# Four attention layers in a row: layers of different batches mixed on every engine, and the full layers' values in fp32

## The reference

```python
def L0(x):   # 32-wide queries and keys, full attention
    Q, K, V = Wq x + bq, Wk x + bk, Wv x + bv
    return gamma * (V @ softmax(Q K^T)^T) + x
def L1(x):   # and L3: 32 groups, 256-wide queries and keys
    h = group_norm(x) * g + b
    q, k, v = wq h + bq, wk h + bk, wv h + bv
    return x + wo (v @ softmax(q^T k / 16)^T) + bo
def L2(x):   # tokens: xs = x as (1024, 256)
    x_ln = ln(xs); q = 8 heads of 32, * 32 ** -0.5; k, v = 32 wide, shared by the heads
    sim = where(causal, -max, q k^T)
    av = ln(softmax(sim) v @ wo + xs)
    ff = gelu(ln(ln(av) @ w1 + b1)) @ w2 + b2
    return ff + av
x = L3(L2(L1(L0(x))))
```

## Time and profile before

| | |
|---|---|
| runs | 1568.68, 1571.64, 1576.68 us |
| the profiled execution | 1572.43 us, its span 1570.7 us |
| TensorE busy | 1326.2 us (84%) |
| VectorE busy | 1008.6 us (64%) |
| ScalarE busy | 567.8 us (36%) |
| GpSimd busy | 122.8 us (8%) |
| DMA | 27.20 MB, 17 GB/s on average |

### The profile page before, as it was taken

The page is one execution under the profiler, slowest core; times in us unless marked ns, Lnnn a source line. Parts: engine busy times, 40 slices in busy tenths (PEclk is TensorE's granted clock), DMA queues, the critical chain, the costliest instruction groups (busy, mean ns, idle before and its releaser), DMA issues.

```text
span 1570.7 us, 21594 instructions
## 1 busy us (share of the span) xinstructions
PE 1326.2 (84%) x7440; PEld 999.4 (64%) x7440; DVE 1008.6 (64%) x1913; ACT 567.8 (36%) x777; POOL 122.8 (8%) x314
## 2 busy tenths in 40 slices
PE   5789888958978988984998898896798898889688
PEld 4568664547866865444876776544686687645577
DVE  2647568666565756866656565877575565696665
ACT  2324224514342423452434331452343242245143
POOL 0000011210000001121000000212000000112100
PEclk9789979989979987997998997998798899799699
DMA  4000110000000011000000003000000001100000
GB/s 140 1 27 1 41 42 2 2 1 1 29 1 27 1 44 39 2 1 1 1 29 1 27 0 82 2 1 1 1 1 29 1 1 38 45 1 2 1 1 27
DMA packets 16393, 27.20 MB, mean 17 GB/s; under 512 B 2576, under 2 KB 6800, under 8 KB 16272
## 3 DMA queue, kind: packets, MB, share of 16 engines
q1 hardware_dynamic: 16272, 25.66, 5.9%
HBM read 8.61 MB, written 4.19 MB: 8 GB/s over the span
## 4 chain that ended last, share of the span: by engine, by line
issue 88%; POOL 7%; PE 4%; POOLq 0%; DVE 0%; ACT 0%
PE ring L589 3%; POOL cprobs L560 3%; POOL rstd L544 2%; POOL idle_pool L559 2%; PE ring L670 0%; POOLq L426 0%; PE ring L738 0%; POOLq L543 0%; PE ring L743 0%; ACT h_hi L974 0%; DVE x L1174 0%; POOLq L547 0%; DVE gn_nb L1250 0%; DVE gn_msc L1249 0%; DVE gn_sc L1248 0%
## 5 line engine op out<-in xcount | busy, mean ns | idle before, releaser
L1030 ACT ACTIVATE cprobs<-ring 128x1024 f32<-128x1024 f32 (+1 forms) x192 | 152.1, 812 | 206.3 <-PE ring L855 205.8
L589 PE MATMUL ring<-probsT_hi,vt_hi 128*128 128x512 f32 x384 | 158.2, 412 | 11.9 <-DVE probsT_lo L1120 11.6
L918 ACT ACTIVATE probsT_hi<-ring 128x1024 fp32r<-128x1024 f32 x96 | 98.1, 1026 | 188.4 <-PE ring L670 188.0
L1120 DVE TENSOR_TENSOR probsT_lo<-ring,probsT_hi 128x1024 fp32r<-128x1024 f32 x96 | 116.5, 1221 | 67.0 <-ACT probsT_hi L918 67.0
L831 PE MATMUL ring<-ks,qs 96*128 96x512 f32 (+3 forms) x384 | 144.0, 452 | 17.9 <-DVE part_max L1375 6.1
L589 PE MATMUL ring<-probsT_hi,vt_lo 128*128 128x512 f32 x384 | 153.9, 401 | 0.0
L589 PE MATMUL ring<-probsT_lo,vt_hi 128*128 128x512 f32 x384 | 153.6, 400 | 0.0
L1375 DVE TENSOR_REDUCE part_max<-ring 128x2 f32<-128x1024 f32 (+3 forms) x128 | 127.3, 1017 | 35.1 <-PE ring L835 17.2
L855 PE MATMUL ring<-qs,ks 98*128 98x512 f32 (+3 forms) x384 | 115.6, 396 | 13.6 <-DVE part_max L1375 12.1
L544 POOL TENSOR_TENSOR rstd<-var_eps,half_neg 128x2 f32<-128x2 f32 (+1 forms) x52 | 46.2, 889 | 997.8 <-DVE var_eps L1245 548.1
L926 ACT ACTIVATE probs<-ring,neg_max 128x1024 f32<-128x1024 f32 x96 | 106.8, 1113 | 42.0 <-DVE neg_max L1154 38.8
(11 more groups left out here) (218 smaller groups left out, 2592.3 us busy)
## 6 DMA issues: line engine op xcount, KB each, us to landing
qs<-q_hi SPq DMA_DIRECT2D x64, 128.0 KB, 2.3
xin<-x_dram SPq DMA_DIRECT2D x4, 1024.0 KB, 5.1
qs<-q_lo SPq DMA_DIRECT2D x32, 128.0 KB, 2.3
out_dram<-x SPq DMA_DIRECT2D x8, 512.0 KB, 2.9
qs<-max_rows SPq DMA_DIRECT2D x64, 4.0 KB
raw_L_wv<-L_wv_dram SPq DMA_DIRECT2D x2, 256.0 KB, 6.2
raw_L_woT<-L_woT_dram SPq DMA_DIRECT2D x2, 256.0 KB, 6.3
raw_L_wq<-L_wq_dram SPq DMA_DIRECT2D x2, 256.0 KB, 6.6
```

Of the source, the lines that this page charges most:

```text
L589: ins = mm(out, w, m, start=first and n == 0, stop=last and n == len(every) - 1)
L918: A(dst, flat(name) if src is None else src, ACT.Identity, bias=bias, scale=scale).then_inc(hi_ready, 1)
L1030: A(causal_probs(step, two, n), slot(event_name(e))[:, :, 0:n], ACT.Exp).then_inc(act_read, 1)
L1120: ins = v.tensor_tensor(dst, src, f32(hi), ALU.subtract)
```

## The change

- **Two chains.** The loop over batches is gone; all work is written out. The *full chain* is the preparation of L0's weights and 12 full layers, in the order of `FULL`, so that full layers of one batch stand beside the causal layer of another. The *causal chain* is the rest of the preparation and the 4 causal layers. On each engine both chains are generators, and a string of `ORDER` says which goes on next (`F` or a digit for a step of the full chain, `C` or a letter for one of the causal; on TensorE digit and letter also give the PSUM bank).
- **PSUM** is 7 single banks that both chains take by these letters, and one bank of sums for the causal values.
- **Values of full layers in fp32.** `vt` and `probsT` are no longer split. `full_values` works in quarters of 256 queries: 2 channel tiles by 8 key tiles, one fp32 product of 256 columns each, 64 for each layer. VectorE's low halves of both are gone; ScalarE copies the transposed tile once.
- **Scaling** of the tiles is done by ScalarE in 9 of the 12 full layers (`SCALED_BY`, `scaled`), by VectorE in 3.
- **Causal layer** in 8 blocks of 256 queries by 4 heads, all 4 heads in one exponent. The feed-forward part is in 4 token parts of 256 (3 before). Each block has its own stack of 12 transfers of 32 partitions by 256 queries; there are 4 places for stacks.
- **Start.** The input is loaded behind L0's weights; the other weights are loaded and prepared in the causal chain, beside the first full layers.

On SP, before, the first transfers of a causal layer are those of the first half of the queries, both groups of heads at once: 12 transfers; 12 more follow for the second half (the last row is their first), and then the first maxima.

The diff, cut to its core (the kernel's other helpers are rewritten as generators around the same instructions):

```diff
+FULL = [("L0", 0), ("L1", 0), ("L0", 1), ("L1", 1), ("L0", 2), ("L3", 0), ("L1", 2), ("L0", 3), ("L3", 1), ("L1", 3),
+        ("L3", 2), ("L3", 3)]
...
+SCALED_BY = ["dve" if n in (0, 1, 11) else "act" for n in range(len(FULL))]
...
+ORDER = {
+    "PE": (
+        "0F2eF02F4Fg02F40Fg24F02FFF3F50F24FFF5F02e6FFF0c3FFF64F024F0F2404F20F42F06FFF4F20F46FFF2F04c6FFF06FFFec0F4F0c"
...
+    events = [("xt", 0), ("xt", 1), ("xn", 0), ("q2", 0), ("kv", 0), ("vt", 0)]
+    events += max_events(0) + max_events(1) + [("shift", 0), ("shift", 1)]
...
+def weave(order, full, causal):
+
+    for ch in order:
+        next(full if ch in "F0123456" else causal)
...
-                    wait_read(sp, b, event_name(("q2", ib)))
...
-                        for g, src in enumerate((q2[0], q2[0], q2[1])):
-                            sp.dma_start(qs[DH * g:DH * (g + 1), ib, a::4, :].bitcast(F32),
-                                         src[DH * a:DH * (a + 1), :, sl].bitcast(F32)).then_inc(stack_in[ib][a // 2], 16)
...
+            def stacks(b, k):
+                hg, qi = BLOCKS[k]
+                wait_read(sp, f"C{b}.q2{qi // 2}")
+                if k >= STACKS:
+                    wait_filled(sp, causal_name(b, last_exp[k - STACKS]))
+                for g, src in enumerate((q2[0], q2[0], q2[1])):
...
+                        sp.dma_start(qs[DH * g:DH * (g + 1), k % STACKS, a, :].bitcast(F32),
+                                     src[DH * a:DH * (a + 1), hg, token_quarter(qi)].bitcast(F32)
+                                     ).then_inc(stack_in[k % STACKS], 16)
+                    yield
...
+            def causal_chain():
+                for b in range(B):
+                    for k in range(STACKS):
+                        yield from stacks(b, k)
+                    yield from shifts(b, 0)
+                    yield from shifts(b, 1)
+                    for k in range(2, K):
+                        yield from shifts(b, k)
+                        if k + 2 >= STACKS and k + 2 < K:
+                            yield from stacks(b, k + 2)
...
-            with sp.Fori(0, B - 1) as b:
...
+            def full_values(l, b, qi):
+                wait_read(pe, full_name(l, b, ("t", 2 * qi + 1)))
+                o = open_unit(full_name(l, b, ("o", qi)))[:, 0, :]
+                for ct in range(CT):
+                    for j in range(NT):
+                        last = mm(o[:, ct * QUARTER:(ct + 1) * QUARTER], vt[:, j, ct * P:(ct + 1) * P],
+                                  probsT[:, qi % (NQ - 1), j, :], start=j == 0, stop=j == NT - 1)
+                        if ct == CT - 1 and j == NT - 1:
+                            last.then_inc(filled["f"], 1)
+                        if j % TPH == TPH - 1:
+                            yield
...
-                    last = product(acc[:, ct, :], [([s[:, j, ct * P:(ct + 1) * P] for s in vt],
-                                                    [s[:, ib, j, :] for s in probsT])
-                                                   for j in range(j0, j0 + TPH)],
-                                   first=j0 == 0, last=j0 + TPH == NT)
...
+            def scaled(n, ti):
+                act.wait_ge(row_sum_inverted, scaled_no(n, ti))
+                A(probs[:, ti % 2, :], probs[:, ti % 2, :], ACT.Identity,
+                  scale=row_inv[:, ti:ti + 1]).then_inc(probs_scaled["act"], 1)
+
+            def turned(l, b, ti):
+                name = full_name(l, b, ("t", ti))
+                wait_filled(act, name)
+                nc.scalar.copy(probsT[:, ti // 2 % (NQ - 1), :, (ti % 2) * P:(ti % 2 + 1) * P],
+                               slot(name).rearrange("p b (s n) -> p (b s) n", n=P)).then_inc(read_done["f", "act"], 1)
...
-                    ap = [s[:, ti // TPH, :, ts] for s in probsT]
-                    lo(b, f"{l}.t{ti}", ap[1], ap[0], slot(f"{l}.t{ti}").rearrange("p b (s n) -> p (b s) n", n=P))
```

More of the change, by code:

```diff
@@ new lines, in full_events, with full_name, max_events @@
+    out += [("t", 0), ("s", 3), ("t", 1), ("s", 4), ("t", 2), ("o", 0), ("s", 5), ("t", 3), ("s", 6), ("t", 4), ("o", 1)]
+    return out + [("s", 7), ("t", 5), ("t", 6), ("o", 2), ("t", 7), ("o", 3)]
+def full_name(layer, b, e):
+    return f"{layer}.{b}.{e[0]}{e[1]}"
+def max_events(k):
+    out = []
+    for t in range(TPQ * BLOCKS[k][1], TPQ * (BLOCKS[k][1] + 1)):
+        end = (t + 1) * P
+        for ch, (lo, hi) in enumerate([(0, end)] if end <= HALF else [(0, HALF), (HALF, end)]):
+            out += [("max", k, t, ch, lo, hi, two) for two in ((2,) if hi - lo <= QUARTER else (0, 1))]
+    return out
@@ new lines, in evenly, with norm, fills @@
+def evenly(events, first, places):
+    return [(first + i * (places - first) // len(events), e) for i, e in enumerate(events)]
+def norm(k):
+    return [("norm", k, i) for i in range(NORM_PIECES)]
+def fills(k, places):
+    ahead = max_events(k + 2) + [("shift", k + 2)] if k + 2 < K else []
+    if k == 0:
+        ahead = [("xn", 1)] + ahead
+    elif k == 1:
+        ahead = [("q2", 1)] + ahead[:2] + [("kv", 1)] + ahead[2:] + [("vt", 1)]
+    out = evenly(ahead, 0, places) if ahead else []
+    part = k // 2 - 1
+    if part >= 0:
+        if k % 2 == 0:
+            late = ([("tg", part - 1), ("w2", part - 1)] if part else [])
+            out += evenly(late, 1, places - 1) if late else []
+            out.append((places - 1, ("wo", part)))
+        else:
+            out += evenly([(e, part) for e in FEED_FORWARD[1:6]], 0, places)
+    return out
@@ L127, in causal_schedule @@
             step += 1
+        fill = fills(k, len(base))
         for i, e in enumerate(base):
             events.append(e)
-            events += [f for at, f in fill[k] if at == i]
+            events += [f for at, f in fill if at == i]
             if divide:
                 events.append(divide.pop(0))
-            if e[0] == "values" and e[1] < k and e[2] == TPH * (blocks[k - 1][1] + 1) - 1:
-                divide = norm(k - 1)
-        assert not divide
-    return events + pending + norm(len(blocks) - 1) + [(e, part) for e in FEED_FORWARD for part in (1, 2)]
@@ L139, in evenly, with is_final @@
-def evenly(events, places):
-    return [(i * places // len(events), e) for i, e in enumerate(events)]
-def norm(k):
-    return [("norm", k, i) for i in range(NORM_PIECES)]
-def event_name(e):
+            if is_final(e):
+                divide += norm(e[1])
+    tail = NQ - 2
+    events += divide + pending + norm(K - 1) + [("tg", tail), ("w2", tail)]
+    return events + [(e, tail + 1) for e in FEED_FORWARD]
+def is_final(e):
+    return e[0] == "values" and e[2] == TPQ * (BLOCKS[e[1]][1] + 1) - 1
@@ L209, in split_units @@
[L209 to L233 removed]
+        return f"C{b}.o{e[1]}"
@@ new lines, in causal_name, with full_units, causal_banks @@
+    return f"C{b}." + ".".join(map(str, e[:4] + e[-1:]))
+FILLED_BY_ACT = ("xt", "shift", "exp", "tg", "w2")
+NO_UNIT = ("norm", "ln2b", "f1b", "f2b")
+def full_units():
+    out = []
+    for l, b in FULL:
+        for e in full_events(l):
+            out.append((full_name(l, b, e), "act" if e[0] in ("s", "t", "v") else "dve", 1 if e[0] in ("gn", "o") else 2))
+    return out
+def causal_banks(e):
+    if e[0] == "max":
+        return 1 if e[-1] == 2 and e[5] - e[4] <= P else 2
+    if e[0] == "exp":
+        return 1 if queries(e[1], e[2]) <= P else 2
+    return 2 if e[0] in ("xt", "xn", "q2") else 1
@@ L590, in product, with both, project @@
                 return ins
-            def output_products(l, out):
+            def both(w):
+                return [lambda i, c, ms=slice(m * P, (m + 1) * P): w[i][:, c, ms] for m in range(CT)]
+            def project(name, weights, src, sl):
+                o = open_unit(name)
+                for bank, w in enumerate(weights):
+                    last = product(o[:, bank, :], [([w(i, c) for i in (0, 1)], [s[:, c, sl] for s in src])
+                                                   for c in range(CT)])
+                last.then_inc(filled[chain[name]], 1)
```

1801 lines of the change are left out of this document (942 added, 859 removed).

## The result

The changed kernel takes 1561.97 us (median of 20 runs), the kernel before 1569.14 (20 runs): ratio 0.995, 95% interval 0.9933 to 0.9966. I had forecast 1470 with a range of 1340 to 1535. The change gains 0.5% where 6.5% were expected, so the prediction was wrong.

The account below looks back on a forecast made before the run. TensorE's work paces the middle of a full layer, one dependent chain the causal tail, group norms and L0. Work 1261 + 13 + 15 + 25 + 12 + 30 + 101 + 12 = 1469, with 1.5 around 1470 us; range 1340 to 1535.

Parts of the forecast that it names:

- Values in fp32: Full layers' values: 64 fp32 products of 0.436 us a layer replace 96 split ones; TensorE gains 71 us of work.
- rival B: TensorE's work is dearer: fp32 products expose weight loads, mixed stretches lose 8% instead of 3%; 1542 us, chance 11%.
- Start: Ahead of the first product: x loads behind L0's weights, then half a cast and half a subtraction; 13 us.
- The queue of SP: Causal layers' starts: products wait for stack transfers at 0.64 us an issue; 101 us, plus 12 of lower clock.
- Rival A: SP's issues are hidden, first shifts do not wait for four stacks, so 101 and 12 drop out; 1358 us, chance 20%.
- VectorE and ScalarE: Busy about 820 and 690 us, both under 60% of the span, hidden behind TensorE.
- Mixing: Stretches where both chains have work: waits cover each other, 3% of the remaining 960 us lost, 30 us.
- end of the last causal layer: One chain only, once L3 of batch 2, beside it, runs out: 25 us of overhead, bounds 10 to 45.
- One chain only, L0 and L1 of batch 0: First two full layers, nothing beside them: 15 us of overhead, as VectorE's part of a tile falls to 2.1 us.
- The small terms: Overheads at the kernel's end: end of the last causal layer 25 us, L3 of batch 3 and the last store 12.
- C: Rival: ScalarE, now scaling tiles, blocks the full chain's transposes, 2 us in each of 96 tiles; 1660 us, chance 6%.

Follow-up runs that it names:

- before_fp32: The kernel before with only the full layers' values in fp32, pieces of 256 columns, VectorE's low halves gone: 1587.08 us, ratio 1.0095.
- wide_stacks: The changed kernel with a batch's first four stacks filled by 12 transfers of 32 x 2 x 512 instead of 48: 1511.7 us, ratio 0.9648 to the kernel before.
- scale_by_vector: The changed kernel with the tiles scaled by VectorE in all 12 full layers, not in 3: 1559.64 us, ratio 0.9913 to the kernel before.
- serial: The changed kernel with its chains not mixed, each layer finished before the next on every engine: 1938.01 us, ratio 1.2368 to the kernel before.
- norm_before_second: Changed kernel, 12 wide first transfers on two queues, plus first token half transposed back before the second half's tokens are taken in: 1492.77 us, ratio 0.9503.

## Why the prediction was wrong, by its own steps

*Values in fp32: right.* 64 products a layer cost 0.424 us each (starts 0.212 apart, two records each), 0.436 was forecast; alone they add 65 us of work (before_fp32). The first half of rival B, that they expose their weight loads, falls by this; its second half, that the mixed stretches lose 8% and not 3%, pointed the right way, and even its 1542 us were too few.

*Start: right.* The first product stands at 13.5 us, forecast 13.

*The queue of SP: right in mechanism, place and size.* 12.0 and 38.6 us behind the query product against 12.6 and 38; the loss of these stretches is 122 us (113 forecast), of it 69.7 the waits for `qs`. The lower clock costs some 37 us around them. Of these 22 lie between query product and first exponent product, where SP's queue sets the time and slow work takes nothing more; 14 lie in the 12 us behind each (12 forecast). wide_stacks takes the larger wait out and gains 50. Rival A, which had 20%, falls. The prediction's "0.64 us in every issue of the trace" was read too widely: of the kernel before's loads from memory at the start most took 0.41 to 0.55 us, and the 0.6 holds for the transfers from SBUF to SBUF, on which the term rests. The Trainium skill's page "DMA: Bandwidth & Descriptors" gives about 50 ns for a transfer's dispatch on the GpSimd path (section on the anatomy of one DMA). No run here issues from GpSimd; for SP's queue the trace shows 0.63 us.

*VectorE and ScalarE: right.* Both stay in the shade (scale_by_vector).

*Mixing: the step that failed.* It said: for the remaining 960 us of work I take 3%, 30 us, since two chains should do better than the 11% that L3 alone shows. It was 105 us, 11% again, a little over the upper bound that I had given (100). The gap between one kernel's waits and another's was never worked out from rows; it was a hope. What the runs show in its place is this. First, waits were not lying there to be filled: serial shows that these events in series lose 653 us where the kernel before loses 363, so the mixing's 376 us for the larger part (290) repay what the regrouped events had given up. Second, on engines with a fixed order a step waits behind the other chain's steps. In the tail of each causal layer, up to the next group norm or query products, 12 to 17 us are lost, four times; three of these tails are some 40 of the 105 us, the fourth is the line "end of the last causal layer". At the end of the three the low half of the normalised tokens, 1.22 us, stood behind the second half's norm and a residual, and TensorE waited 4.8 us; moving that step took most of this wait away, but about two thirds of it came back elsewhere, and the 9 us of the median, though as forecast, are partly luck (norm_before_second). Third, the other 60 us or so are spread over the long stretches between the stacks and the tails: 240 to 461, 588 to 848, 956 to 1185 and 1285 to 1437 us of the span hold 43 us of idle time, in gaps of at most 3.7 us (several behind ScalarE's exponents, some at the group norms of full layers), and 13 us of the lower clock's cost. No experiment touched these, so why the mixed stretches lose 11% is shown for the tails in part and open for the rest.

*One chain only, L0 and L1 of batch 0: mis-sized.* 34.6 us for 15. TensorE's idle time in the two layers is some 13 us, 6.3 of them at L1's group norm, which has nothing beside it, and the lower clock costs another 13 (the first 6 us of products run at it: 0.43 us between starts, and 0.23 from 19.6 us on). I had counted on VectorE's shorter tile and left the clock out.

*The small terms* at the end came within 9 us. With the work and the first product they are 9 us less than forecast in all, against 20 and 9 us more in the two lines above.

The forecast's form hid the risk: 406 us of waits and clock before, 208 after, with 198 as the gain. Measured by busy time it is 363 and 272. The largest gain was a difference of two large numbers, one of them guessed, and its bounds (10 to 100) left no reason for a value near the lower end: their middle, 55, makes the sum 1494, their upper end 1539. The chance left outside the range was also added up too low: C and the outer halves of A and B are 6 + 10 + 5.5 = 21.5%, not 17.

## What to carry to other kernels

When chains are mixed, price the new order's waits from the traced chains' own waits until an experiment shows less, and ask how much of them the old order already hides. Count transfers per batch, not bytes: in this kernel every issue delayed all behind it on its queue, and moving one forward only changed who waited. Where a product needs two late inputs, only the later one is worth shortening. A named wait that shrinks is not yet time won: look at the total idle time, and at other kernels with the same edit.

## What the runs showed of the hardware

- An issue on SP of a transfer from SBUF to SBUF took mostly 0.61 to 0.65 us, for 2, 4, 32 and 128 KB alike (single groups of 8 up to 0.79 each); one on ScalarE's queue took the same (4 in 2.58 us), and ScalarE's next work stood behind it. Most loads from memory at the start took 0.41 to 0.55 us.
- fp32 products of 256 columns started 0.212 us apart on average at full clock (1508 records without the waits), though each comes with weights of its own.
- The lower clock's cost went with TensorE's idle time, though not strictly: 199 us of cost at 454 us idle, 122 at 241, 99 at 213, 68 at 201, 75 at 197, 82 at 189, 60 at 159, 49 at 148.
